# Attention values multiplied ahead by U2[1], and the running sum kept in SBUF by GpSimd, in a four-layer graph network kernel

## What is computed

```python
def _L1_gnn_ref(X, S, W1, W2, W3, U1, U2, ln_g, ln_b):
    R = S + jnp.eye(N); R = R / R.sum(-1, keepdims=True)
    Z = jnp.zeros_like(X); Xf = X; Xa = X
    for n in range(2):
        A = _top_p_attention(Xa, W1, W2, W3)      # softmax of q k^T, nucleus 0.9, rows sum to 1
        Xf = R @ Xf
        Xa = A @ Xa
        Z = Z + Xf @ U1[n].T + Xa @ U2[n].T
    h = X + Z
    mu = h.mean(-1, keepdims=True)
    var = jnp.mean((h - mu) ** 2, axis=-1, keepdims=True)
    return (h - mu) / jnp.sqrt(var + 1e-5) * ln_g + ln_b
```

## Time and profile before

| | us |
|---|---|
| three timed runs, median (lowest to highest) | 1008.23 (1007.75 to 1008.57) |
| the profiled execution's own time | 1006.43 |
| its span in the trace | 1004.6 |
| TensorE busy, share of the span | 804.8 (80%) |
| VectorE | 666.2 (66%) |
| ScalarE | 474.7 (47%) |
| GpSimd | 68.8 (7%) |

### The profile page before, as it was taken

The page is one execution under the profiler, slowest core; times in us unless marked ns, Lnnn a source line. Parts: engine busy times, 40 slices in busy tenths (PEclk is TensorE's granted clock), DMA queues, the critical chain, the costliest instruction groups (busy, mean ns, idle before and its releaser), DMA issues.

```text
span 1004.6 us, 11941 instructions
## 1 busy us (share of the span) xinstructions
PE 804.8 (80%) x3886; PEld 551.0 (55%) x3886; DVE 666.2 (66%) x2092; ACT 474.7 (47%) x945; POOL 68.8 (7%) x63
## 2 busy tenths in 40 slices
PE   4879984988888865786898788685598999994994
PEld 4844432756666654683575565565295585542342
DVE  5967858488777689734979876788596022245715
ACT  4886334336545556344435646846944241024111
POOL 0020001010000000000000000201001000013001
PEclk9889986988988996989897888899799999997898
DMA  9849502543103100000253300601342819100001
GB/s 336 331 165 432 214 10 84 168 167 126 44 1 125 44 1 2 1 2 0 84 175 117 128 1 1 226 1 53 130 172 70 321 41 427 63 1 0 1 0 42
DMA packets 20219, 108.23 MB, mean 108 GB/s; under 512 B 1824, under 2 KB 8752, under 8 KB 9776
## 3 DMA queue, kind: packets, MB, share of 16 engines
q1 hardware_dynamic: 18752, 106.77, 28.6%
q10 hardware_dynamic: 1392, 0.61, 0.3%
HBM read 88.23 MB, written 19.14 MB: 107 GB/s over the span
## 4 chain that ended last, share of the span: by engine, by line
PE 49%; DVE 25%; ACT 12%; issue 9%; DMA 2%; POOL 1%; DVEq 1%; POOLq 0%; SPq 0%; ACTq 0%
PE PS L802 9%; PE PS L671 6%; DVE AT L1518 6%; PE PS L607 6%; PE PS L541 5%; PE PS L724 4%; PE PS L871 4%; DVE mxv L1657 4%; ACT BC L1243 3%; DVE nd L1521 3%; PE PS L1052 3%; PE PS L1028 3%; ACT AT L1243 3%; DVE AT L2100 3%; PE PS L1058 2%
## 5 line engine op out<-in xcount | busy, mean ns | idle before, releaser
L1074 ACT ACTIVATE AT<-PS 128x512 f32<-128x512 f32 (+2 forms) x240 | 118.7, 559 | 121.3 <-PE PS L541 86.8
L541 PE MATMUL PS<-ident,AT 128*128 128x128 f32 x544 | 85.8, 293 | 38.5 <-DVE rS L2169 18.9
L1657 DVE TENSOR_REDUCE mxv<-PS 128x1 f32<-128x2048 f32 x32 | 73.2, 2288 | 56.7 <-PE PS L724 56.6
L724 PE MATMUL PS<-K,ST 64*128 64x512 f32 x256 | 87.9, 779 | 13.6 <-ACT EA L1211 7.7
L541 PEld LDWEIGHTS PS<-ident,AT 128*128 128x128 f32 x544 | 69.0, 152 | 46.9 <-DVE rS L2169 20.1
L2100 DVE MAX8 AT<-AT 128x8 f32<-128x256 f32 (+2 forms) x336 | 92.7, 347 | 0.7
L802 PE MATMUL PS<-AT 128*128 128x128 f32 x512 | 72.1, 291 | 13.1 <-ACT AT L1074 12.6
L802 PE MATMUL PS<-hr,AT 128*128 128x128 f32 x512 | 71.3, 289 | 8.2 <-ACT AT L1074 7.4
L802 PEld LDWEIGHTS PS<-AT 128*128 128x128 f32 x512 | 65.7, 202 | 21.9 <-ACT AT L1074 17.7
L802 PEld LDWEIGHTS PS<-hr,AT 128*128 128x128 f32 x512 | 65.0, 200 | 17.3 <-ACT AT L1074 11.2
L1074 ACT ACTIVATE ST<-PS 128x512 f32<-128x512 f32 (+3 forms) x43 | 23.9, 561 | 104.6 <-PE PS L1058 24.3
(11 more groups left out here) (297 smaller groups left out, 1370.5 us busy)
## 6 DMA issues: line engine op xcount, KB each, us to landing
AT<-keep_at SPq DMA_DIRECT2D x32, 1024.0 KB, 5.0
EA<-in_adj SPq DMA_DIRECT2D x20, 1024.0 KB, 6.5
keep_at<-AT SPq DMA_DIRECT2D x8, 2048.0 KB, 25.0
AT<-keep_at SPq DMA_DIRECT2D x8, 2048.0 KB, 12.4
AT<-in_adj SPq DMA_DIRECT2D x12, 1024.0 KB, 6.6
EA<-keep_degrees SPq DMA_DIRECT2D x1, 1024.0 KB, 6.5
keep_x<-K SPq DMA_DIRECT2D x4, 256.0 KB, 6.8
out<-EA SPq DMA_DIRECT2D x4, 256.0 KB, 2.3
```

The lines of the kernel that those rows point to most:

```text
L541: return pe.transpose(dst, src, ident[0:p, 0:p])
L724: return pe.matmul(bank(to + n), ST[1][half_rows, k * P:(k + 1) * P], keys[half_rows, n * BK:(n + 1) * BK], start=True, stop=True)
L1074: return act.activation(dst, src, ACT.Copy)
L1657: v(dve.tensor_reduce(mxv[:, odd:odd + 1], PS[:, b:b + 4, :], AX.XY, ALU.max))
```

## The change

In step one `projected` issues a single matmul of 256 columns: the transposed result times U2[0] and U2[1] side by side. ScalarE copies the first half to `T` and the second half over the result in `xa_rows`; the transposed result itself stays in `xaT` for keys and queries. In step two attention is applied to these multiplied values, and ScalarE's scaled result in `T` is what is to be added to the sum; the transposes, copies and projections of step two are gone. GpSimd adds into `R` in SBUF: two tiles at a time `hr` or `XR` (`own_added`), and tile by tile `T` (`attended_added`), at fixed places of its program. A new semaphore `z_sum` counts the finished sums and takes the place of `z_ok` where the sum itself is waited for; ScalarE also waits for it before it writes `T` anew. The last block's `T` is added by VectorE in `normed_pair`, with the row sums. For the other blocks the row sums are taken by ScalarE in `first_norm`, by a copy of `R` with accumulation.

```diff
             def result_turned(step, g, k):
...
-                pe.wait_ge(q_out, min(gi + 3, NB + 1 if step == 0 else 2 * NB))
-                src = xa_rows[:, G * g + k, :] if step == 0 else T[:, k, :]
-                turn(bank(7)[:, 0:P], src).then_inc(ex_turned, 1)
+                pe.wait_ge(q_out, min(gi + 3, NB + 1))
+                turn(bank(7)[:, 0:P], xa_rows[:, G * g + k, :]).then_inc(ex_turned, 1)
 
             def projected(step, g, k):
                 pe.wait_ge(exT_ok, G * (NB * step + g) + k + 1)
-                aT = xaT[:, (G * g + k) * P:(G * g + k + 1) * P] if step == 0 else xa2T[:, k * P:(k + 1) * P]
-                pe.matmul(bank(7)[:, P:2 * P], aT, WT[:, U2T + step, :], start=True, stop=False)
-                pe.matmul(bank(7)[:, P:2 * P], ident[:, :], R[:, G * g + k, :], start=False, stop=False)
-                mm = pe.matmul(bank(7)[:, P:2 * P], ident[:, :], (hr if step == 0 else XR)[:, G * g + k, :],
-                               start=False, stop=True)
+                aT = xaT[:, (G * g + k) * P:(G * g + k + 1) * P]
+                mm = pe.matmul(bank(7)[:, P:3 * P], aT, WT[:, U2T:U2T + 2, :].rearrange("p m c -> p (m c)"),
+                               start=True, stop=True)
                 mm.then_inc(z_mm, 1)
...
@@ GpSimd
+            def own_added(u):
+
+                p, c = u // UNITS, u % UNITS
+                pair = slice(2 * c, 2 * c + 2)
+                pool.wait_ge(un_z, u + 1)
+                if p == 1:
+                    pool.wait_ge(z_sum, NT)
+                pool.tensor_tensor(R[:, pair, :], R[:, pair, :], (hr if p == 0 else XR)[:, pair, :], ALU.add)\
+                    .then_inc(pre_ok, 1)
+
+            def attended_added(gi):
+
+                pool.wait_ge(pre_ok, G // 2 * (gi + 1))
+                for k in range(G):
+                    t = G * (gi % NB) + k
+                    pool.wait_ge(z_ok if gi < NB else ex_ok, G * gi + k + 1)
+                    pool.tensor_tensor(R[:, t, :], R[:, t, :], T[:, k, :], ALU.add).then_inc(z_sum, 1)
+
+            ADDED = {1: range(0, 6), 2: range(6, UNITS), 5: range(UNITS, UNITS + 6), 6: range(UNITS + 6, 2 * UNITS)}
+            ATTENDED = {2: (0,), 3: (1, 2, 3), 6: (NB,), 7: (NB + 1,)}
...
@@ ScalarE, result_out (step one only) and attend
-                    dst = xaT[:, (G * g + k) * P:(G * g + k + 1) * P] if step == 0 else xa2T[:, k * P:(k + 1) * P]
-                    copy(dst, bank(7)[:, 0:P]).then_inc(exT_ok, 1)
...
+                    copy(xaT[:, t * P:(t + 1) * P], bank(7)[:, 0:P]).then_inc(exT_ok, 1)
+                    act.wait_ge(z_mm, c + 1)
+                    if g > 0:
+                        act.wait_ge(z_sum, c + 1 - G)
+                    copy(T[:, k, :], bank(7)[:, P:2 * P])
+                    copy(xa_rows[:, t, :], bank(7)[:, 2 * P:3 * P]).then_inc(z_ok, 1)
...
+                if step == 1:
+                    act.wait_ge(z_sum, c + 1 - G)
                 act.activation(dst, bank(6)[:, 0:P], ACT.Copy, scale=rS[:, g % 2, k:k + 1]).then_inc(ex_ok, 1)
...
@@ ScalarE, first_norm
-                act.wait_ge(z_ok, NT + G * (b + 1))
+                act.wait_ge(z_sum, NT + G * (b + 1))
...
+                for k in range(G):
+                    t = b * G + k
+                    act.activation(hr[:, t, :], R[:, t, :], ACT.Copy, accum_out=rs[:, t:t + 1]).then_inc(rs_ok, 1)
+                act.wait_ge(rs_ok, G * (b + 1))
...
@@ VectorE, normed_pair
-                dve.wait_ge(z_ok, NT + t0 + 2)
+                dve.wait_ge(pre_ok, 2 * UNITS)
+                dve.wait_ge(ex_ok, NT + t0 + 2)
+                for k in range(2):
+                    v.put(stt(R[:, t0 + k, :], T[:, 2 * h + k, :], 1.0, ALU.mult, R[:, t0 + k, :], ALU.add,
+                              accum_out=rs[:, t0 + k:t0 + k + 1]))
+                v.wait()
+                dve.sem_inc(z_sum, 2)
```

More of the change, by code:

```diff
@@ L430, in _ @@
             back(5)
-            sp.wait_ge(z_ok, 2 * NT)
+            sp.wait_ge(z_sum, 2 * NT)
             for u in (4, 6, 3, 2):
@@ L810, in attend @@
                     rows_turned(normed, k - 1)
-                if k > 0:
+                if k > 0 and step == 0:
                     result_turned(step, g, k - 1)
@@ L827, in attend @@
                 mults(3)
-                if k == G - 1:
+                if k == G - 1 and step == 0:
                     result_turned(step, g, k)
```

48 lines of the change are left out of this document (26 added, 22 removed).

## The result

The changed kernel takes 992.3 us in the median of four runs (984.7 to 992.8) where the kernel before, timed beside it, takes 1008.4: a ratio of 0.983 with a 95% interval of 0.9802 to 0.9859. The forecast was 995.1 us, range 989.5 to 1003.0. Sign, mechanism and range held. The sum of the forecast did not hold as well as the time: the additions cost more than it said, the gain was larger still, and the two partly cancelled. Which term of the gain was too small is only in part known.

A forecast was written before the change was run, and what follows sets the result against it. No single engine bounds the kernel; TensorE (49% of the chain) and VectorE (25%) take turns. Gains of 16.7 us, less 0.7 on ScalarE and 2.9 for additions, give -13.1 us: 995.1 us from 1008.23, range 989.5 to 1003.

The forecast's parts named there:

- ScalarE's 0.7: Added ScalarE cost of first-norm row sums, blocks 4 and 5: 0.2 us spilling plus 0.4 to 0.5 us, +0.7 us.
- tiles: Blocks 4 to 7: TensorE paces the tiles, so removed projections gain 2.6 us in block 4, 2.0 in each later block.
- the cold piece: Block 4: one of the three removed projections ran at TensorE's low clock, 1.29 us instead of 0.67.
- tails: Last tiles of blocks 4 to 7: next work no longer waits for transpose, copies and projection; 2.6, 2.0, 0.5, 1.2 us.
- The row sums: ScalarE's four new row sums before each first norm of blocks 4 to 6: 0.39 us each, 1.6 us a norm, partly hidden.
- Step one's term: Blocks 0 to 3: TensorE paces eight projections, each one 128-column matmul shorter; 8 x 0.22 = -1.8 us.
- 0.19 us each for fifteen: GpSimd additions where VectorE paces: some 15 delay VectorE by 0.19 us each, +2.9 us in all.
- My own sign: VectorE's 128x2048 operations stay near 2.35 us in the mean; forecast wrong if that grows by more than 0.1 us.
- Rival 2: Step two's tiles are paced by ScalarE's copies, so only the tails gain: 1005.5 us, chance 0.12.
- Rival 3: Norm chain costs in full, 1.4 us of row sums plus 2.4 us late GpSimd addition: 998.9 us, chance 0.17.
- Rival 4: GpSimd additions hold the port for 1.20 us per 128 columns, kernel slower: 1019.8 us, chance 0.09; decides from 0.70 us.
- Block 6's chain: Block 6's tail from result through row sums, norms and scaling to TensorE's next work: 7.5 us instead of 7.97.

The follow-up runs named there:

- experiment 9: Changed kernel with the first six own-part additions of each step and step two's last two moved to where VectorE has slack: 987.72 us, ratio 0.9812 to before.
- experiment 3: Changed kernel with step two's serial block tails (transpose, copy, three matmuls, copy) put back and waited for: 998.34 us, +9.9 us at equal clock against the changed kernel.
- experiment 4: Changed kernel with step one's additions back on TensorE as identity matmuls, step two as changed: 993.88 us, +1.8 us at equal clock against the changed kernel.
- experiment 2: Changed kernel with three unawaited 128-column matmuls put back in the second to fourth tile of blocks 4 to 7: 997.92 us, +6.5 us at equal clock.
- experiment 8: Changed kernel with one of the four ScalarE row sums left before each first norm of blocks 4 to 6: 988.04 us, +0.3 us at equal clock.
- experiment 6: Changed kernel with each of GpSimd's 44 additions done three times (add, subtract, add): 1000.73 us, +7.6 us at equal clock against the changed kernel.
- experiment 5: Changed kernel with all 44 GpSimd additions cut to one column per tile, waits kept: 992.25 us, -3.2 us at equal clock against the changed kernel.

## Why the prediction was right, and where it was not

**The gross gain was too small, and the excess is not traced to a term.** With the additions out of the way (experiment 9) the kernel is 19.5 us (+-1.3) under the one before at equal clock (15.5 + 4.1); the forecast's gains less ScalarE's 0.7 were 16.0 us. In step two the terms were nearly right: tiles 8.0 forecast (2.6 + 2.0 for each later block, less the cold piece) and 6.5 (+-1.3) measured; tails 8.0 (without the row sums) and at most 9.9 (+-1.3), since experiment 3's wait behind block 7 is longer than it was before. The row sums, 2.3 us in the forecast, are not seen: taking three quarters of them away gave nothing (+0.3 +-1.6).

Step one's term, eight tiles and -1.8 us, agrees with the chain of both traces. The distances of block 2 do follow TensorE, as experiment 4 shows, but VectorE ends last behind them. If each of the 16 tiles counted, experiment 4's two units more would cost 16 x 0.45 = 7.2 us, and the additions that it saves would have to give back 5.4 us, more than all 44 cost. Eight tiles make it 3.6, and 1.8 us given back.

Together the terms make at most 1.8 + 6.5 + 9.9 = 18.2 us before any row sums, against 19.5. The difference lies within the intervals, so it may be nothing. One part was priced at nothing in the forecast, and no run put it back: ScalarE's two copies for each tile of step two that is not the last of its block, 24 in all.

**The additions cost more than 2.9 us, and others than I thought.** The step "0.19 us each for fifteen" took its number from an operation of 2.35 us that was lengthened. The sum of the shifts is 5.2 us at nine places, 3.2 to 4.1 us (+-1.7 and 1.5) of the time. Little of it is from the additions of attended results, which make up 28 of the 44: it is from the additions of 256 columns, above all where three of them stand back to back beside a chain of 128x4 operations, and two of those wait out one addition each. Operations of 128x4 carry 4.0 of the 5.2 us. Three of 128x2048 carry the other 1.2, 0.31 to 0.47 us each where I had taken 0.19. My own sign, the mean of the 128x2048 operations (at most 0.06 us more in any group), held and looked at the smaller part.

**The rivals.** Rival 2 (only the tails gain) is excluded by experiment 2. Rival 3 (the norm chain in full) is excluded in its row sums by experiment 8; ScalarE waits 0.32 us for GpSimd ahead of block 4's scaling, not 3:

```profile
649.42 1.65 ACT L1349 ACTIVATE R<-R,ri,es 128x128 f32<-128x128 f32 x4 [0.32 <-POOL ri L479]
```

Rival 4 asked for 0.70 us a unit of 128 columns: an undisturbed addition takes 0.45 us, one of 256 columns 0.72, and 26 of the 44 lengthen no operation of VectorE. Block 6's chain, forecast at 7.5 us against the 7.97 of the earlier trace rows, is 7.19 us, since the row sums follow each other in 0.30 us and not 0.39.

**Signs.** The 96 instructions fewer, block 7's distance of 5.9 us and the query beside the result came as said.

**The median.** At equal clock 15.5 us (+-1.0) are measured against 13.1. A gross gain 3.5 us larger, less additions 1.2 us dearer (4.1 against 2.9), gives that by construction, since the gross gain was worked out from the 15.5. So the mechanism held, with each tested term within about 2 us of its forecast, but that the median came within 2.8 us is in part luck: two errors of opposite sign. The rest is within the spread of the clock.

## What to carry to other kernels

Work that is moved to GpSimd is cheap or dear by what VectorE does at that moment: hang it on a semaphore that marks a slack of VectorE, and keep it away from chains of tiny operations that another engine waits for. The distance of two equal events tells which engine paces them, but not what a saving there is worth: look at what the engine waits for behind the stretch, since a shorter distance can come back as a longer wait. Where runs of one kernel differ by 5 us, plot time against TensorE's granted clock before explaining 2 us; and where TensorE waits long ahead of its own serial work, something to do in that wait kept the clock up here, though no gain in the total was shown.

## What the runs showed of the hardware that I had not expected

- VectorE's 128x4 operations with one tensor as input (TENSOR_SCALAR) wait for a GpSimd addition like those with two: 0.65 instead of 0.17 us at 218.04 us. A RECIPROCAL of the same size, at 532.02 us in experiment 6, ran 0.17 us beside an addition.
- GpSimd's addition costs 0.45 us at 128x128 and 0.72 at 128x256, so by estimate about 0.27 us for 128 columns and 0.18 for itself; a 128x2 addition that met a 2.35 us operation of VectorE took 2.19 us.
- Executions of one program differ by up to 13 us (991.85 to 1005.18 in experiment 2) with the clock that TensorE gets after its waits, and an edit that only shortens the work of another engine seems to move that clock: 0.882 in the mean of five executions in experiment 5, 0.889 in ten of the changed kernel.
